# Weight quantisation of all six pairs on VectorE instead of alternately on VectorE and GpSimd

## The reference, cut to what matters

```python
def ternary_quant(w_fp32, g=64):
    w = w_fp32.astype(bfloat16)
    w_g = w.reshape(-1, g)
    scale = clip(mean(abs(w_g), axis=-1, keepdims=True), 1e-08, None)
    q = clip(round(w_g / scale), -1, 1)
    w_hat = (q * scale).reshape(w.shape)
    return w + stop_gradient(w_hat - w)

gu = einsum('bsd,hd->bsh', x, ternary_quant(w_gate_up))     # 2048 x 256 weights
gate, up = split(gu, 2, axis=-1)
hn = rms_norm(silu(gate) * up)
out = einsum('bsh,dh->bsd', hn, ternary_quant(w_proj))      # 256 x 1024 weights
...
x = x + tanh(g_xattn[0]) * wkv(w, u, layernorm(x), ctx)
x = x + tanh(g_ffn[0]) * ternary_ffn(layernorm(x))
x = x + tanh(g_xattn[1]) * attention(layernorm(x), ctx, mask)
x = x + tanh(g_ffn[1]) * fp8_linear(layernorm(x))
```

## Time and profile before

| | before |
|---|---|
| runs, us | 187.92, 187.33, 185.48 |
| median, us | 187.33 |
| profiled execution, span, us | 183.6 |
| VectorE busy | 146.5 us, 80% |
| TensorE busy | 121.2 us, 66% |
| GpSimd busy | 92.3 us, 50% |
| ScalarE busy | 74.5 us, 41% |
| chain that ended last, by engine | VectorE 53%, issue 16%, TensorE 13% |

### The profile page before, as it was taken

How to read it: one execution, slowest core, us unless ns; L and a number is a source line. 1 busy time by engine, 2 the same in 40 slices (tenths; PEclk the granted TensorE clock), 3 DMA queues, 4 the chain that set the end, 5 groups by cost and what they waited for, 6 DMA issues and landing times.

```text
span 183.6 us, 2132 instructions
## 1 busy us (share of the span) xinstructions
PE 121.2 (66%) x720; PEld 78.1 (43%) x726; DVE 146.5 (80%) x260; ACT 74.5 (41%) x126; POOL 92.3 (50%) x94
## 2 busy tenths in 40 slices
PE   6869952831297561546409955998788858789363
PEld 6757722620163220111205633544356726666242
DVE  0477998999986099999999998679999588891840
ACT  2325727664094131230003813764568113650631
POOL 5195353979600485685960964583826240520050
PEclk9978995695559968555966999999999999999999
DMA  3699800000000000000000000000000000000033
GB/s 95 179 359 363 250 2 2 0 0 0 0 0 4 0 0 2 0 2 0 0 0 0 0 4 0 2 0 0 0 4 0 0 0 4 0 0 0 2 114 118
DMA packets 8045, 6.90 MB, mean 38 GB/s; under 512 B 2273, under 2 KB 7778, under 8 KB 8034
## 3 DMA queue, kind: packets, MB, share of 16 engines
q1 hardware_dynamic: 7602, 6.75, 11.4%
q10 hardware_dynamic: 432, 0.00, 0.1%
HBM read 5.71 MB, written 1.05 MB: 37 GB/s over the span
## 4 chain that ended last, share of the span: by engine, by line
DVE 53%; issue 16%; PE 13%; POOL 5%; DMA 5%; ACT 4%; SPq 1%; POOLq 1%; DVEq 0%; ACTq 0%
DVE xn L1036 7%; DVE GR L1156 6%; DMA wgu_raw<-in_L_ffn_w_gate_up_dram 5%; DVE xs L1076 4%; DVE hbuf L1150 4%; DVE stats L1024 4%; DVE wsign L1107 3%; DVE wsign L1126 3%; DVE SV L1060 3%; DVE S L1046 2%; DVE wmask L1125 2%; PE ps L825 2%; PE ps L804 2%; PE ps L805 2%; DVE wmask L1132 1%
## 5 line engine op out<-in xcount | busy, mean ns | idle before, releaser
L804 PE MATMUL ps<-xhi,wT 128*128 128x512 f16 x64 | 26.8, 419 | 19.4 <-DVE hbuf L1150 15.9
L805 PE MATMUL ps<-xlo,wT 128*128 128x512 f16 x64 | 27.1, 423 | 0.0
L596 ACT ACTIVATE wgu_raw<-hbuf 128x512 f16<-128x512 f32 x16 | 10.0, 626 | 41.7 <-DVE hbuf L1150 41.6
L804 PEld LDWEIGHTS ps<-xhi,wT 128*128 128x128 bf16 x64 | 6.7, 104 | 30.6 <-DVE hbuf L1150 18.7
L1036 DVE TENSOR_SCALAR xn<-xs,mv,rstd 128x256 f32<-128x256 f32 x24 | 17.3, 770 | 2.2 <-POOL rstd L373 2.1
L825 PE MATMUL ps<-wT,wgu_raw 128*128 128x256 bf16 x64 | 15.4, 283 | 5.1 <-DVE GR L1156 2.4
L1024 DVE BATCH_NORM_STATS2 stats<-xs 128x6 f32<-128x256 f32 x32 | 12.2, 409 | 6.8 <-DMA xs<-in_x_dram 6.6
L1156 DVE TENSOR_TENSOR GR<-hbuf,wgu_raw 128x512 f16<-128x512 f32 x16 | 16.5, 1030 | 0.0
L463 POOL TENSOR_TENSOR sqsum<-sqsum,S 128x512 f32<-128x512 f32 x8 | 11.5, 1435 | 7.8 <-ACT S L599 7.5
L825 PE MATMUL ps<-wT,GR 128*128 128x256 bf16 x64 | 15.3, 282 | 0.0
L1150 DVE SCALAR_TENSOR_TENSOR hbuf<-ps,pscale,sil 128x512 f32<-128x512 f32 x16 | 11.9, 746 | 3.8 <-ACT sil L591 2.1
(11 more groups left out here) (156 smaller groups left out, 330.6 us busy)
## 6 DMA issues: line engine op xcount, KB each, us to landing
wgu_raw<-in_L_ffn_w_gate_up_dram SPq DMA_DIRECT2D x4, 512.0 KB, 8.8
xs<-in_x_dram SPq DMA_DIRECT2D x2, 512.0 KB, 7.9
ctx_sb<-in_ctx_dram SPq DMA_DIRECT2D x2, 512.0 KB, 8.7
wp_raw<-in_L_ffn_w_proj_dram SPq DMA_DIRECT2D x1, 1024.0 KB, 10.1
out_dram<-xs SPq DMA_DIRECT2D x4, 256.0 KB, 2.3
wlin_raw<-in_L_ffn_weight_dram SPq DMA_DIRECT2D x1, 256.0 KB, 9.2
bias_bc<-in_L_ffn_bias_dram SPq DMA_DIRECT2D x1, 128.0 KB, 9.5
mask_u<-in_mask_BxS_bk_dram SPq DMA_DIRECT2D x2, 32.0 KB, 7.9
```

What stands on the lines that cost most here:

```text
L596: act.activation(hhi[:, h, j, :], hbuf[:, b, :], ACT.Copy).then_inc(hhi_ready, 1)
L804: pe.matmul(ps[:, 4 + 2 * b + up, :], w, xhi[:, h, c, :], start=(c == 0), stop=False)
L805: mm = pe.matmul(ps[:, 4 + 2 * b + up, :], w, xlo[:, h, c, :], start=False, stop=(c == CH - 1))
```

## The change: what it does

The subtraction, addition and product of pairs 1, 3 and 5 move from GpSimd to VectorE, nine instructions of 128 x 1024 bf16. `quant_there_0`, `quant_there_1` and `quant_mask` are gone; all pairs use `quant_here_0` and `quant_here_1`, and the hand-over semaphores go with them. The steps also stand at other places: pair 0's last two steps and all four of pair 1 stand behind the absolute value of pair 4, pair 3 stands whole in the loop's step n = 1, and pair 5 whole in step n = 5.

```diff
-        POOL_PAIRS = (1, 3, 5)
...
-            def quant_there_0(p):
-                b = p % 2
-                pool.wait_ge(wsc_ready, p + 1)
-                pool.wait_ge(wsum_ps, p + 1)
-                if p >= 2:
-
-                    pool.wait_ge(wq_ready, p - 1)
-                pool.tensor_tensor(wmask[:, b, :], wscale[:, p, :], wabs[:, p, :], ALU.subtract).then_inc(wdiff_ready, 1)
-
-            def quant_there_1(p):
-                b = p % 2
-                pool.wait_ge(wmask_ready, POOL_PAIRS.index(p) + 1)
-                link(pool.tensor_tensor(wmask[:, b, :], wabs[:, p, :], wmask[:, b, :], ALU.add))
-                pool.tensor_tensor(wmask[:, b, :], wmask[:, b, :], wsign[:, b, :], ALU.mult).then_inc(wmag_ready[1], 1)
...
-            quant_there_0(1)
             wkv_products(2)
             wkv_products(3)
...
             power_and_shift(1, 0, TPC, 1)
-            quant_there_1(1)
...
             pool.partition_all_reduce(gmax_all[:, :], gmax[:, :], P, bass.bass_isa.ReduceOp.max).then_inc(gmax_done, 1)
-            quant_there_0(3)
-            quant_there_1(3)
...
                     if h == 0 and j == 1:
-                        quant_there_0(5)
...
                     if h == 0 and j == 2:
-                        quant_there_1(5)
...
-            def quant_mask(p):
-
-                b = p % 2
-                dve.wait_ge(wdiff_ready, POOL_PAIRS.index(p) + 1)
-                dve.tensor_tensor(wsign[:, b, :], wmask[:, b, :], wabs[:, p, :], ALU.is_lt).then_inc(wmask_ready, 1)
...
             weights_abs(4)
-            quant_mask(1)
+            quant_here_1(0)
+            quant_here(1)
             weights_clip(3)
             wkv_denominator(2, wkv_weights(2))
             ln_apply(1, TPC // 2, TPC // 2, 1)
             weights_abs(5)
             weights_clip(4)
-            quant_here_1(0)
             weights_clip(5)
...
             power_of_two()
-            quant_mask(3)
             for n in range(CHUNKS * HT):
...
                 if n == 1:
                     quant_sign(2)
+                    quant_here(3)
                     quant_sign(3)
                     wkv_values(2)
                 if n == 2:
                     wkv_values(3)
-                    quant_mask(5)
                     quant_here(4)
                     quant_sign(4)
...
                 if n == 5:
                     ln_apply(1, TPC + TPC // 2, TPC // 2, 2)
+                    quant_here(5)
                     quant_sign(5)
```

More of the change, by code:

```diff
@@ L215, in gated_blocks @@
         wsc_ready = sem("wsc_ready")
-        wmask_ready = sem("wmask_ready")
-        wdiff_ready = sem("wdiff_ready")
         wsign_ready = sem("wsign_ready")
-        wmag_ready = [sem("wmag_ready_dve"), sem("wmag_ready_pool")]
+        wmag_ready = sem("wmag_ready")
         wq_ready = sem("wq_ready")
@@ L1105, in quant_sign @@
                 b = p % 2
-                dve.wait_ge(wmag_ready[p in POOL_PAIRS], sum((q in POOL_PAIRS) == (p in POOL_PAIRS) for q in range(p + 1)))
+                dve.wait_ge(wmag_ready, p + 1)
                 dve.tensor_scalar(wsign[:, b, :].bitcast(U16), wT[:, p, :].bitcast(U16), 0x8000, None,
@@ L1129, in quant_here_1 @@
                 b = p % 2
-                dve.wait_ge(own_mask, p // 2 + 1)
+                dve.wait_ge(own_mask, p + 1)
                 after(step(dve.tensor_tensor(wmask[:, b, :], wabs[:, p, :], wmask[:, b, :], ALU.add)))
-                dve.tensor_tensor(wmask[:, b, :], wmask[:, b, :], wsign[:, b, :], ALU.mult).then_inc(wmag_ready[0], 1)
+                dve.tensor_tensor(wmask[:, b, :], wmask[:, b, :], wsign[:, b, :], ALU.mult).then_inc(wmag_ready, 1)
             def quant_here(p):
```

## The result

The change makes the kernel faster by 5.8%. It ran at 175.69, 176.37, 175.49 and 176.72 us, median 176.03; the kernel before, beside it, at 187.92, 187.33, 185.48 and 185.62, median 186.48. The ratio is 0.942 [0.935, 0.949]. The same kernel timed again later, beside other runs of the kernel before, gave 175.75 us and 0.947 [0.942, 0.951]. The forecast was 177.5 us in 172.6 to 182.8.

What follows compares the result with a forecast made beforehand. VectorE bounds the loop's first part, first waiting for GpSimd, then full, much of it lengthened by GpSimd's instructions. Entry -6.1 and loop -3.7 make -9.8: span 183.6 to 173.8, median 187.33 to 177.5 us, range 172.6 to 182.8.

Steps and rivals of the forecast that it cites:

- The entry: Start of the feed-forward loop: VectorE's 5.91 us wait for GpSimd goes, `ffn_mul(0)` from 64.64 to about 58.5, -6.1 us.
- the thin cover: GpSimd's second changeover, ending near 58.5, would delay nobody: bias needed only in the last block, first square at about 60.
- Ahead of the loop: Before the loop: five added VectorE instructions +3.5, layer norms -3.6, comparison's wait -0.7; sum -0.8 us.
- The place for pair 0's two instructions: Ahead of the loop, VectorE waited 0.52 us for ScalarE's scales, so moving these two away from there gains nothing.
- The loop: Inside the loop up to `xn_low(1)`: seven added instructions +4.9, removed waits on GpSimd 8.6, net -3.7 us.
- The step that I had called the weakest: In the loop: waits caused by GpSimd's kept sums, WKV products and weight parts stay, though some fall on other instructions.
- The refund around GpSimd's removed six: In the loop, VectorE instructions lengthened beside six GpSimd instructions shorten: 1.5, 1.8, 1.7, 1.8 and 1.8, together 8.6 us.
- The tail: Behind `xn_low(1)` nothing of the change is left: the remaining 69.5 us move as a block.
- A: Waits change seat: all seven instructions added in the loop cost 1.64 instead of 0.70, +6.6; 184.1 us; 9%.
- B: TensorE at the low clock becomes the bound in the loop from `ffn_mul(3)`; gain some 5 smaller, 182.5 us; 12%.
- C: Slower: long durations belong to VectorE's own instructions, nothing is refunded, the nine cost 1.75 each; 197.2 us; 4%.
- D: Wait not removed: `ffn_mul(0)` hangs on the changeover through the reduction and `pscale`; about -3.7 remains, 183.6 us; 3%.

Runs made afterwards that it cites:

- the filled kernel: The change, with pairs 0's and 1's sign steps ahead of the last clip and pair 2's first two steps ahead of `ffn_mul(0)`: 173.71 us, again 173.79.
- the ghosts: The change plus nine unused GpSimd subtractions that read SBUF, at the places of the old nine, nobody waiting for them: 188.82 us, ratio 1.017.
- The wait alone: Kernel before, all nine instructions still on GpSimd; only pair 3's comparison and sign step move later, behind `ffn_mul(0)`: 183.19 us, ratio 0.988.
- memset ghosts: The change plus two unused GpSimd memsets, which read nothing, in place of each of nine added GpSimd subtractions: 176.87 us, ratio 0.951.

## Why the prediction was right, point by point

**The entry.** Idle time gone, TensorE's `up` next, `ffn_mul(0)` at 58.37 against 58.5. That the changeover would go on at no cost ahead of the bias was read from the earlier trace rows and held. The sentence that the wait was no cost of the subtraction goes too far: VectorE was ready at 58.12, L383 began at 61.89 and took 2.11, so 3.8 of the 5.9 us were the changeover and 2.1 the subtraction itself. The sum did not need the difference, since the change takes both out of VectorE's way. The bias came at 59.29; the first sum waited 1.24 us for ScalarE behind it, so the thin cover held.

**Ahead of the loop.** -1.0 against -0.8. The place for pair 0's two instructions was free, as the 0.52 us of the earlier trace rows had said. I had credited 0.7 for the comparison at 33.8; it fell by 0.86.

**The loop.** The sum came out for the right reason, 3.4 against 3.7. VectorE's busy time between `ffn_mul(0)` and the end of `xn_low(1)` fell from 48.71 to 45.03 us, 3.7, and its idle time grew by 0.3. The step that I had called the weakest, that the remaining waits stay as they are, did fail in the seats and held in the sum. Pair 3's subtraction took 1.75 and pair 5's subtraction and comparison 1.75 and 1.52, beside GpSimd's sums and weight parts. These are waits that stood on other instructions before. Pair 3's replaces the 1.49 us of a sign step (74.13 us before), which now takes 0.43; pair 5's two replace 1.49 and 1.52 (106.12 and 107.64 us before), which now take 0.43 and 0.69. 3.0 us moved, none was added. The refund around GpSimd's removed six was worked out as 8.6 from five durations. Pair 4's part of it looks different: its product fell to 1.65, not to 0.69, and its subtraction from 1.75 to 0.68 instead. The sum is 8.6 again. That the span came out to 0.1 us is partly luck: the stretches were off by 0.2, 0.3 and 0.1 us, and the first and the third made up for the second.

**The tail** moved as a block, 69.4 against 69.5, in both traces of the change. The experiments show that this was no law: it took 70.4 to 70.8 in the three kernels with one pair on GpSimd and in the filled one, and 69.4 again in the kernel with the WKV products moved, where `xn_low(1)` ends at the same time as in one trace of the filled one.

**The rivals.** A: three of seven instructions in the loop were lengthened, but by waits that left other places, so the cost was nothing. B: it did not cost the 5 us, but it was close. VectorE was busy 8.15 of the 8.42 us ahead of 104.42, TensorE 4.73, at a clock of 0.59. TensorE, with the change:

```profile
99.55 0.39 PE L799 MATMUL ps<-wT,wgu_raw 128*128 128x256 bf16 x1 [4.71 <-DVE wT L1084]
...
104.31 0.27 PE L799 MATMUL ps<-wT,GR 128*128 128x256 bf16 x1
104.53 0.38 PE L778 MATMUL ps<-xhi,wT 128*128 128x512 f16 x1
```

It stood idle 4.71 us until VectorE had quantised pair 5, and was done with the projections it then owed at about the moment when `xn_low(1)` ended: `gate_up(8)` starts 0.11 us behind it. So VectorE still set the time, with no idle time of TensorE between in this trace and 0.20 us in the second trace of the change. In the filled kernel `gate_up(8)` starts 0.43 behind `xn_low(1)` (101.95), and there B's price is the 0.3 us. C was refuted by the ghosts, D by the entry.

**My expectations that missed.** Pair 1 back on GpSimd: 1.6 and 2.0 us instead of 0.8 to 1.0; in the one trace the rest is TensorE's clock at `up` of n = 0 and a longer tail, and what sets that clock stays open. Pair 3 back: 1.4 too high, since I had taken the whole 5.91 us as pair 3's, when the first changeover behind pair 1 carried a part. Pair 5 back: 0.9 too low, by the tail. The wait alone: 183.19 us against 182 to 183.

## What to carry to other kernels

Before work is shared out between VectorE and GpSimd, compare what the move spares VectorE with what GpSimd's instruction costs it while it runs: here an instruction of 0.69 us was handed to an engine that needed 2.1 to 2.5 us for it and held VectorE for up to 1.8 us meanwhile, so taking back nine of them made the fullest engine less full. In a timeline the sign is one line that takes 0.69 us at one place and 2.2 to 2.5 at another and ends some 0.55 us behind GpSimd's instruction (70.00 against 69.45 in the kernel before). When a wait is removed, look at what the waited-for engine still has to do: alone, the wait's removal kept 3.1 of 5.2 us.

## What I had not expected of the hardware

- Memsets on GpSimd need no changeover behind the reduction. In the kernel with memset ghosts they follow it at once (51.93 us, 0.82 long; the first memset at 52.49), and the 7.00 us of "issue" come only ahead of the next ordinary instruction:

```profile
51.93 0.82 POOL L420 PARTITION_ALL_REDUCE gmax_all<-gmax  x1 [5.83 <-issue]
52.49 1.12 POOL L373 MEMSET E<- 128x1024 f32 x1
...
57.87 0.95 POOL L374 MEMSET E<- 128x1024 f32 x1
65.82 0.47 POOL L424 TENSOR_SCALAR bias_g<-bias_bc,tg 128x256 f32<-128x256 f32 x1 [7.00 <-issue]
```

- The changeover is 5.64 to 5.83 us to the reduction and 6.54 to 7.59 back from it, where a trace shows it as "issue", and it is no cost as long as it starts in time: with the change the reduction starts at 51.18, when its input is there, behind 8.06 us of idle time. What GpSimd does in a changeover no trace here shows.
- One instruction of GpSimd can hold VectorE for less than its length where both have more to do: VectorE's 1.63 to 1.65 us per step of pair 4 alternate with GpSimd's products and sum of 1.59 to 1.71, so about 0.95 is added by each, and not 1.6.
- TensorE's granted clock can fall late in an execution, far behind the place that was changed. From 138 to 142 us it is 0.67 and 0.61 in the two traces of the filled kernel and 0.57 in the one with the sums moved, and 1.00 with the change. The time of arrival does not decide it: the kernel with the WKV products moved ends `xn_low(1)` at 101.02, as one trace of the filled kernel does (101.01), and has 1.00 there; the memset ghosts end it at 104.16, close to the change, and have 0.60 from 142 to 146. What does decide it stays open, and differences of 1 to 1.5 us between these kernels can come from it alone.
